# Self-attention, shared expert and routed experts of a transformer block written as one program per engine, with the routing and weight splits moved and one routed tile fewer

## The reference, cut to what matters

```python
x = x + xattn(layernorm(x), ctx)      # 16 heads, key size 64, layer norm behind
x = x + attn(layernorm(x))            # self-attention, 16 heads of 16, rotary
x = x + ffn(layernorm(x))             # one shared expert, 8 routed, top 2

def ffn(xf):                                          # 4096 x 256
    gates = sigmoid(xf @ Wg)                          # 8 experts
    vals, idx = top_k(gates, 2); vals = vals / vals.sum(-1)
    w = zeros(T, 8).at[arange(T), idx].add(vals)
    shared = silu(xf @ Ws1) * (xf @ Ws3) @ Ws2        # 256 -> 512 -> 256
    h = silu(xf @ We1[e]) * (xf @ We3[e])             # for every expert e
    routed = sum over e of w[:, e] * (h @ We2[e])
    return (shared + routed) / 3
```

## Time and profile before

| | us |
|---|---|
| median of 3 runs | 2243.11 (2242.41 to 2248.22) |
| the profiled execution, its own time | 2244.75 |
| its span, first to last instruction | 2243.0 |
| PE busy in the span | 2121.4 (95%) |
| VectorE (DVE), ScalarE (ACT), GpSimd (POOL) busy | 1594.3, 1282.7, 707.9 |
| mean granted clock of PE | 0.983 of full speed |

### The profile page before, as it was taken

One profiled execution on the slowest core, in us unless ns is written; L12 is line 12 of the kernel. 1 busy time (PEld: TensorE's weight loads), 2 busy tenths in 40 slices (PEclk: granted clock), 3 DMA queues, 4 the chain that ended last, 5 costly groups with the idle time before them and its releaser, 6 DMA issues. The chain is left out here.

```text
span 2243.0 us, 48623 instructions
## 1 busy us (share of the span) xinstructions
PE 2121.4 (95%) x16836; PEld 1862.6 (83%) x16837; DVE 1594.3 (71%) x2992; ACT 1282.7 (57%) x3071; POOL 707.9 (32%) x677
## 2 busy tenths in 40 slices
PE   7999999999999999999999999788986996999997
PEld 6888898898888888888888887667775885888886
DVE  6767767767767768768778676678885655666665
ACT  5556556556556556656656655456664334555554
POOL 5001001011011011011011011567772374677775
PEclk9999999999999999999999999899998998999999
DMA  4001001001001011010010001432224321333333
GB/s 149 12 18 34 14 19 33 14 19 33 12 21 33 2 31 32 1 33 23 9 33 23 9 10 44 163 133 75 77 88 146 95 76 38 52 56 52 55 54 43
DMA packets 103215, 104.41 MB, mean 47 GB/s; under 512 B 14064, under 2 KB 92656, under 8 KB 103152
## 3 DMA queue, kind: packets, MB, share of 16 engines
q1 hardware_dynamic: 87280, 84.62, 11.9%
q0 software_dynamic: 15872, 18.95, 5.3%
HBM read 72.73 MB, written 30.81 MB: 46 GB/s over the span
## 5 line engine op out<-in xcount | busy, mean ns | idle before, releaser
L893 PE MATMUL banks<-ctxT_hi,qk_hi 128*128 128x256 f32 x1024 | 301.1, 294 | 0.0
L893 PE MATMUL banks<-ctxT_hi,qk_lo 128*128 128x256 f32 x1024 | 290.0, 283 | 0.0
L893 PE MATMUL banks<-ctxT_lo,qk_hi 128*128 128x256 f32 x1024 | 288.7, 282 | 0.0
L542 ACT ACTIVATE probs<-banks,nbias 128x256 f32<-128x256 f32 x512 | 236.2, 485 | 69.8 <-DVE nbias L677 69.4
L549 ACT ACTIVATE pc<-banks 128x512 f32<-128x512 f32 x256 | 153.0, 598 | 192.0 <-PE banks L893 187.2
L635 DVE TENSOR_TENSOR qk_lo<-banks,qk_hi 128x512 fp32r<-128x512 f32 x256 | 165.8, 686 | 69.9 <-ACT qk_hi L504 69.8
L893 PE MATMUL banks<-pT_hi,ctx_hi 128*128 128x512 f32 x512 | 206.2, 403 | 4.8 <-DVE qk_lo L635 3.1
L430 POOL TENSOR_TENSOR rstd<-mv,power 128x2 f32<-128x2 f32 x32 | 22.2, 693 | 589.0 <-DVE mv L718 589.0
L635 DVE TENSOR_TENSOR pT_lo<-banks,pT_hi 128x512 fp32r<-128x512 f32 x256 | 164.7, 684 | 57.0 <-ACT pT_hi L504 56.4
L893 PE MATMUL banks<-pT_hi,ctx_lo 128*128 128x512 f32 x512 | 201.9, 394 | 0.0
L893 PE MATMUL banks<-pT_lo,ctx_hi 128*128 128x512 f32 x512 | 200.7, 392 | 0.0
(11 more groups left out here) (258 smaller groups left out, 6065.6 us busy)
## 6 DMA issues: line engine op xcount, KB each, us to landing
ctx_raw<-in_ctx_dram SPq DMA_DIRECT2D x64, 256.0 KB, 2.7
experts_w<-in_L_ffn_We_dram SPq DMA_DIRECT2D x24, 512.0 KB, 8.3
x_in<-in_x_dram SPq DMA_DIRECT2D x16, 256.0 KB, 2.9
x_again<-in_x_dram SPq DMA_DIRECT2D x16, 256.0 KB, 2.9
x_stream<-z SPq DMA_DIRECT2D x16, 256.0 KB, 2.2
s_x<-x_stream SPq DMA_DIRECT2D x32, 128.0 KB, 2.1
s_x_again<-x_stream SPq DMA_DIRECT2D x32, 128.0 KB, 2.1
x_normalised<-s_xl SPq DMA_DIRECT2D x32, 128.0 KB, 1.7
```

The lines of the kernel that those rows point to most:

```text
L542: nc.scalar.activation(probs[:, s % 2, p, :], scores[:, s % 2, p // 2, (p % 2) * SK:(p % 2 + 1) * SK], ACT.Exp, bias=nbias[:, s % 2, p:p + ...
L893: last = nc.tensor.matmul(out, a, b, start=(n == 0), stop=(n == 3 * len(pairs) - 1))
```

## The change

One `nc.Block()` holds all four parts, so every engine runs them one behind the other and no barrier is left; semaphores take the place of both. PSUM is no longer given out anew for each part: the shared expert uses `banks[1]` for the rises and counts and `banks[0]` for the downs, and the routed experts lay theirs over the same banks.

- **Ahead of the barrier's place.** SP loads `x` of group 0 behind pair 15 (`ahead.load`, to a place of its own). ScalarE copies the upper halves of w1, x0, w3 and w2 behind pair 15, after tile s=0 and s=1 of pair 16, and in pair 17. VectorE subtracts w1's behind s=0 of pair 16, and x0's, w3's and w2's behind all its self-attention work. GpSimd's constants (memsets, iotas) are made behind pair 16. PE does both rises of strip 0 between pair 16 and pair 17. SP's loads of group 1 and of the residual wait, in its order, for the last stores of self-attention.
- **Routing.** `count()` now stands in strip 3 between the rises and `down(2)`; the two empty pieces are gone, so the last piece is in strip 7 instead of 9.
- **Splits.** w1 and half of w3 (12 experts' matrices) are split in the second and third strip of each group from the third group on; w3 of experts 4 to 7 between the shared and the routed part, for the last of which ScalarE waits until all downs are done.
- **Table.** GpSimd reads the table itself, on its own DMA queue, when its 64 DMAs have landed, casts the tokens, and gathers the first four tiles. PE transposes the first routed tile between `down(30)` and `down(31)`.
- **Routed buffers** lie over spent ones (w3_hi over routing's temporaries and shared weights, others over `x`, `x_hi` and `h` of the shared part); the first addition to the output waits for the stores of the shared part, the second tile's first rise for `add_y` of the last group.
- **RT is 71**; the last turn of the loop has 7 tiles.

Core of the diff (the re-indented bodies are otherwise the same):

```diff
@@ self_attention
+            if g.kind == NT // 2 - 1:
+
+                wait_filled(sp, g, ("v", 0))
+                for s in range(2):
+                    sp.wait_ge(x3T_stored[s], 16 * (QT // 2 + 1))
+                ahead.load(sp)
+        wait_freed(sp, Pair(NT // 2 + 1, NT // 2 + 1), ("gate", 0))
...
+            if g.kind == NT // 2:
+                ahead.pool(pool)
...
+                if g.kind == NT // 2 - 1 and s == 1:
+                    ahead.act(act, 0)
+                if g.kind == NT // 2:
+                    ahead.act(act, 1 + s)
+                if g.kind == NT // 2 + 1 and s == 0:
+                    ahead.act(act, 3)
...
+                if g.kind == NT // 2 and s == 0:
+                    ahead.dve(dve, 0)
+        for k in range(1, 4):
+            ahead.dve(dve, k)
...
+            if g.kind == NT // 2:
+
+                pe.wait_ge(shifted_done, NT)
+                ahead.pe(pe)
...
-RT = TOP * TOKENS // P + E
+RT = TOP * TOKENS // P + E - 1
...
-COUNTED_BY = 4
-assert RT % U == 0
+COUNTED_BY = 3
+ROUNDS = -(-RT // U)
...
+SPLIT_UPPER = [i for i in range(2 * FC, STRIPS) if i % FC in (1, 2)]
@@ shared_expert, ScalarE
-                    if f == 2:
-                        copy(w1_hi[:, q], w1[:, q].bitcast(F32)).then_inc(w1_hi_done, 1)
+            if i in SPLIT_UPPER:
+                w, raw, e = split_of(SPLIT_UPPER.index(i))
+                if w is w3_hi:
+
+                    act.wait_ge(routed, 1)
+                copy(w[:, e], raw[:, e].bitcast(F32)).then_inc((w1_hi_done, w3_hi_done)[w is w3_hi], 1)
@@ PE
+        for i in range(STRIPS):
+            if i:
+                for j in range(2):
+                    rise(pe, i, j)
+            if i == COUNTED_BY:
+                count()
+            if i:
+                down(pe, i - 1)
@@ routed_experts, GpSimd
+        nc.gpsimd.dma_start(table[:, :, :], table_dram.rearrange("(p j) c -> p j c", p=P)).then_inc(table_in, 16)
+        pool.wait_ge(table_in, 16)
+        pool.sem_inc(pool_past, 1)
+        nc.gpsimd.tensor_copy(tokens[:, :], table[:, :, 0]).then_inc(tokens_done, 1)
+        pool.wait_ge(tokens_done, 1)
+
+        pool.wait_ge(shares.h3_done, FC * (QUADS - 1))
...
+                if g.first and s == 0:
+
+                    for i in range(2):
+                        pool.wait_ge(shares.stored[i], 16 * QT * QUADS // 2)
@@ ScalarE
+        x_upper(0, 1)
+        for e in range(E // 2, E):
+            if e == E // 2:
+
+                act.wait_ge(shares.sent, 16 * TOP * NT)
+            if e == E - 1:
+
+                act.wait_ge(shares.down_done, QT * STRIPS)
+            nc.scalar.activation(w3_hi[:, e], w3[:, e].bitcast(F32), ACT.Identity).then_inc(shares.w3_hi_done, 1)
@@ VectorE
+        x_lower(0, 1)
+        for e in range(E // 2, E):
+            dve.wait_ge(shares.w3_hi_done, e + 1)
+            nc.vector.tensor_tensor(w3[:, e], w3[:, e].bitcast(F32), w3_hi[:, e], ALU.subtract).then_inc(shares.w3_lo_done, 1)
+        shares.add_last(dve)
@@ PE
+        transpose_x(0, 1)
+        shares.last_down(pe)
+        pe.wait_ge(shares.routed, 1)
+        pe.wait_ge(shares.h_done, STRIPS)
+        pe.wait_ge(shares.w1_lo_done, E)
...
+                    if g.first and s == 0 and j == 1:
+                        pe.wait_ge(shares.w3_lo_done, E)
+                    if g.first and s == 1 and j == 0:
+
+                        pe.wait_ge(shares.y_out, NT)
@@ transformer_block
-        with ExitStack() as both:
...
+        with nc.Block() as block:
+            @block.sync
+            def _(sp):
+                cross.sync(sp)
+                attend.sync(sp)
+                shares.stage.sync(sp)
```

More of the change, by code:

```diff
@@ L48 @@
 Stage = namedtuple("Stage", "sync gpsimd scalar vector tensor")
+Ahead = namedtuple("Ahead", "load pool act dve pe")
 class Region:
@@ L1163, in pair_order, with self_attention @@
     return out
-def self_attention(nc, ctx, t, x1_dram, x2_dram, xl_dram, xT_dram, logits, ident, early, ring, scores, load_ahead):
+def self_attention(nc, ctx, t, x1_dram, x2_dram, xl_dram, xT_dram, logits, ident, early, ring, scores, load_ahead, ahead):
     def sb(name, shape, dt=F32, room=early):
@@ L1467, in scalar @@
                 act_step(act, g, s)
+                if g.kind == NT // 2 - 1 and s == 1:
[4 more added lines that the diff above has]
+                    ahead.act(act, 3)
+                    wait_freed(act, g, ("gate", s))
     chain = [0, 0]
@@ L1730, in __init__ @@
         self.at, self.first, self.last = at, first, last
+        self.tiles = RT - U * (ROUNDS - 1) if last else U
 def load_shared(sp, t, shared, loaded):
@@ L2374, in transformer_block @@
     logits = small.take("logits", [P, NT, E])
+    lists = Region(nc, small.at, 1632)
     empty = small.take("empty", [P, RT, 2])
@@ L2399, in load_ahead @@
             load_experts(sp, t, (w1, w3, w2), part, experts_in)
[L2401 to L2436 removed]
+        banks = [ctx.enter_context(nc.psum_tensor(f"banks{i}", [P, 4, 512], F32)) for i in range(2)]
         low = Region(nc, early, EARLY_ROOM)
@@ L2440, in transformer_block @@
         rest = low.at
-        shared_expert(nc, ident, low, Region(nc, upper, upper_room), shared, shared_in, w1, w1_hi, experts_in, x2, xT, table,
-                      out, logits, slots_empty, expert_of)
-        routed_experts(nc, ident, Region(nc, rest, EARLY_ROOM // 2), Region(nc, upper, upper_room),
-                       Region(nc, spare, 12 * 1024), w1_hi, xl, table, out, (w1, w3, w2), experts_in, expert_of)
+        w3_hi = Region(nc, upper, upper_room).take("experts_w3_hi", [P, E, DC, F], F32R)
@@ new lines, in transformer_block @@
+        experts = ((w1_hi, w1), (w3_hi, w3))
+        shares = shared_expert(nc, ctx, ident, early, low, Region(nc, upper, SPLIT_LATE), Region(nc, upper + SPLIT_LATE, 12 * 1024),
+                               shared, shared_in, experts, experts_in, x2, xT, table, out, logits, slots_empty, expert_of, banks)
+        routes = routed_experts(nc, ctx, ident, rest, lists, Region(nc, spare, 12 * 1024), xl, table, out, experts, w2,
+                                expert_of, banks, shares)
+        attend, opening = self_attention(nc, ctx, t, x1, x2, xl, xT, logits, ident, Region(nc, early, EARLY_ROOM),
+                                         banks[0], banks[1], load_ahead, shares.ahead)
```

1087 lines of the change are left out of this document (543 added, 544 removed).

## The result

| | before | after |
|---|---|---|
| median of the runs, us | 2242.76 (2239.39 to 2248.22, 4 runs) | 2219.23 (2216.98 to 2219.6, 4 runs) |
| the profiled execution, its own time | 2244.75 | 2216.98 |
| its span | 2243.0 | 2215.2 |
| mean granted clock of PE | 0.983 | 0.988 |

A forecast was written before the change was run, and what follows sets the result against it. It took PE to bound the routed loop and later strips, VectorE routing, and a GpSimd chain the second handover. 17.8 us earlier at tile 1 plus 4.9 for one tile made 22.7, so 2220.4 us; range 2214 to 2228.

The forecast's parts named there:

- Front, 5.0: First barrier: strip 0's rises move into self-attention's last wait, so `h` of strip 0 starts 5.0 us earlier.
- Routing, 38.8: Shared part: from `h` of strip 0 to the last routing piece 38.8 us instead of 47.3, with eight strips for ten.
- I give back 0.5: Strip 3: `count` ahead of `down(2)` makes PE wait for the second choice and delays strip 4's `h`; 0.5 us allowed.
- Rival B: Front's gain lost through late loads, or `down(2)` behind `count` costs several us; routing ends 4 to 5 later, 2225; chance 0.15.
- 64 DMAs, 88.9, landing 2.4: GpSimd's table DMAs keep their pace: 88.9 us from first start to last, the last landing 2.4 us later.
- Table read 3.2, cast 0.4: Behind the last table DMA: GpSimd's own table read takes 3.2 us and its cast 0.4, then index copy 0.
- Index copy 0 to tile 1's first product, 16.8: Second handover: the order is as before, so this way still takes 16.8 us and tile 1 comes 17.8 earlier.
- D: Routed loop: GpSimd becomes the bound as its index copies meet VectorE's work; slower, 2284 us; chance 0.03.
- PE stands 3.5 ahead of `down(31)`: Second handover: PE, transposing tile 0 first, waits some 3.5 us for its gather, and its clock may fall.
- One tile, 4.9: Routed loop: one tile less saves one turn of 4.886 us, and the tail behind the last tile is unchanged.
- C: The semaphores replacing the barriers wait as long, so only the tile is gained: 2238.2 us, within 0.3%; chance 0.04.
- A: Second handover: PE's own path with the weights ends last; tile 1's first product 22.9 us earlier, 2215.3 us; chance 0.12.

The follow-up runs named there:

- e4: Changed kernel with routing as before: count behind down in strip 4, two empty pieces back, last piece in strip 9; 2223.51 us (0.9915).
- e2: Changed kernel with the counting matmuls behind `down(2)` instead of ahead of it, still in strip 3; 2214.59 us (0.9873).
- e1: Changed kernel with RT = 72 again, nothing else altered; 2223.17 us (0.9907).
- e6: Kernel before with only the routing moved: count ahead of `down(2)` in strip 3, no empty pieces, barriers kept; 2241.58 us against 2241.89.
- e5: Changed kernel with only the first 32 of 64 table DMAs, so the second half of the tokens gets no routed part; 2217.45 us (0.9891).
- e3: Changed kernel with PE's two rises of strip 0 behind pair 17 instead of between pairs 16 and 17; 2218.77 us (0.9895).
- e7: Kernel before without VectorE's eight w3 subtractions behind the second barrier, w3's lower parts left out; 2241.14 us, one run.

## Why the prediction was right, and which terms were off

The forecast's chain is the one that the trace shows, and e4 shows that it sets the handover. The median lies 1.2 us from the forecast. But terms were off in both directions, and that the match is so close is luck: one error of 2.2 us and one of 2.7 nearly cancel.

- **Front, 5.0:** measured 5.7. The rises took 4.7 us (forecast 4.42), tile 31's way from transposes to logits 1.7 (2.46), so the logits were out at +7.7, where I had +8.2; the rest up to `h` of strip 0 took 3.2 (3.4). The condition on x0's load held: ScalarE copied x0 at 1695.59, and VectorE's subtraction started at 1699.23, right behind the layer norm.
- **Routing, 38.8:** measured 41.0, the term that ran over most. The sum of two strips less was good: 38.3 without any stop, and e2 has 38.0. What failed is "I give back 0.5" for `count` ahead of `down(2)`: it was 3 (e2). I had seen that PE waits for the second choice, but not that the wait is 3.14 us, that its clock then is down for the downs that it passed, and that VectorE, which routing hangs on, waits as long for the next strip. Rival B had "several us" for this, so the range held it. `h` of strip 31, +147.8 for +146.6, is the same stop.
- **64 DMAs, 88.9, landing 2.4:** 88.2 and 2.5.
- **Table read 3.2, cast 0.4:** from the landing of the last table DMA to index copy 0 are 3.5 us, forecast 3.6. But the parts differ: 0.29 and 2.19 for the read, 0.81 for the cast. The gather's 2.89 was too much for the transfer, and the cast met VectorE. The estimate of 2.2 from the Trainium skill (DMA: Bandwidth & Descriptors, Anatomy of one DMA) agrees with the 2.19. Between the last landing and the read the forecast left out 5.8 us of barrier without naming what filled them; it was GpSimd's drain.
- **Index copy 0 to tile 1's first product, 16.8:** 14.1. "The order is as before" was the step that failed. The copies and gathers had run under VectorE's subtractions, and the change moves these (1.7 with the small changes of the gathers); PE's wait for them moved too, from ahead of tile 1's transposes to ahead of tile 0's second product (0.6); and the lower clock held for less of tile 0's products (0.4). I had used the rule on the pair against the change (D), and rows 6 and 8 stood side by side: an index copy of 1.12 inside the 9.16. That part was to be had from the rows.
- **PE stands 3.5 ahead of `down(31)`:** 1.8, and 1.5 more ahead of the second tile. The clock fell behind the first of these stops, as I thought it might, to 0.50 from 1851.5 to 1858.1.
- **One tile, 4.9, the tail the same:** e1 agrees. From tile 1 to the end the traces differ by 6.2, a turn of 4.87 and 1.3 more. The 1.3 isn't the change: the steady turn is 4.86 us in both, and the trace before has two long ones, 5.49 from tile 8 to 9 and 6.21 from 16 to 17, where the changed one has one of 5.34. e6, with the loop of the kernel before, has a mean turn of 4.860 and none of these. What makes a single turn long isn't shown.
- **Rivals.** C and D didn't come: no wait in the chain is put down to the new semaphores, and the loop's pitch is the old one. A was near: the path through PE and the w3 splits, 11.4 from `h` of strip 31 in my working and 12.4 in e5, ends 0.7 to 0.9 us before the chain. I set it aside because GpSimd's DMAs can't shrink, but a gain of 1 us on that side already meets it. With A's path 1.0 longer and `h` of strip 31 1.2 later than I had them, its 2215.3 was out of reach.

Against the forecast, the end lies 3.2 us earlier in the stretch behind the last layer norm: −0.7 front, +2.2 routing, −0.7 DMAs, −2.7 index copies, −1.3 loop. The routing and the index copies, the two terms that I missed, nearly cancelled, and the loop's 1.3 is chance. With the 1.9 us ahead of the change the profiled span is 5.1 below the forecast's 2220.3; the median is only 1.2 below its own, because the profiled execution was the fastest of the four.

## What to carry to other kernels

When an operation is moved ahead of other work on its engine, price not the wait alone but what the engine's clock does behind it, and who waits for the work that was passed: with a wait of 3.1 us ahead of `down(2)` the chain was 3 us longer than with the same matmuls one place later. When a barrier goes, two chains that it had hidden come to the surface together, so ask of each gain how far it carries until the next one ends last; here it was 0.7 to 0.9 us. Look in the trace for what a barrier waits: the second one here waited, with the work done, for a drain of GpSimd of 5.3 us. And where an instruction's duration varies in the trace, find with what it overlaps before taking a stretch over "as before".

## What the runs showed of the hardware that was not expected

- How far the meeting of small GpSimd copies with VectorE's two-input subtractions reaches: 0.18 to 0.19 us alone, 0.69 to 1.12 beside the eight of the kernel before and e6, 0.38 to 0.64 beside the late four of the changed kernel, e1, e3 and e4. Two such copies made the way to tile 1's first product 1.4 us longer; the other 1.4 of e7's 2.8 came by PE's wait and its clock.
- PE's granted clock was at its lower level (0.50 of full) for 3.3 us behind the stop of 3.14 us, and stayed at the upper one with the stop of 1.72 (e2). It also fell behind stops of 1.79 and 1.96 in the changed kernel, so the length of the stop isn't all that counts.
- GpSimd's drain at the end of the shared part's block took 5.30 us in all three traces that have it there (before, e6, e7), longer than any other engine's there (TensorE's weight load 1.67, ScalarE 0.66, VectorE 0.72).
- In two jobs PE, ScalarE and VectorE stopped for up to 43 us in the strips with no releaser in the trace, and all kernels that ran there were longer, the one before by 54 us; unexplained.
